# An attention and ternary-FFN block on one core: the hand-written order of every engine's list laid out anew

## The reference

```python
# attention, 16 heads of 16, latent of 64
xn = layernorm(x)
q = xn @ Wq
latent = (xn @ Wk + xn @ Wv) @ W_down_kv
k, v = latent @ W_up_k, latent @ W_up_v
scores = clip(q k^T / 16) * exp(-1e-4 * |i - j|)
y = softmax(clip(scores)) v @ Wo
x1 = x + layernorm(y)
# feed-forward: Hadamard turn, 4-bit activations, ternary weights
xh = layernorm(x1) @ H
s = max(|xh|) / 7 per token
z = clip(round(xh / s), -8, 7) * s @ ternary(weight).T
out = x1 + layernorm(z)
```

## Time and profile before

| | |
|---|---|
| time, median of 3 runs | 1435.21 (1431.94 to 1436.89) |
| profiled execution, time and span | 1435.05, span 1433.2 |
| mean granted TensorE clock | 0.983 |
| busy: PE, DVE, ACT, POOL | 1349.5, 1179.9, 1098.2, 834.7 |
| first score unit of iterations 0, 16, 31 | 33.72, 701.38, 1331.91 |

### The profile page before, as it was taken

How to read it: one execution, slowest core, us unless ns; L and a number is a source line. 1 busy time by engine, 2 the same in 40 slices (tenths; PEclk the granted TensorE clock), 3 DMA queues, 4 the chain that set the end, 5 groups by cost and what they waited for, 6 DMA issues and landing times.

```text
span 1433.2 us, 35971 instructions
## 1 busy us (share of the span) xinstructions
PE 1349.5 (94%) x12330; PEld 600.5 (42%) x12330; DVE 1179.9 (82%) x2739; ACT 1098.2 (77%) x1125; POOL 834.7 (58%) x1238
## 2 busy tenths in 40 slices
PE   5889999999999999999999999999999999999863
PEld 3334444444444444444444444444444444443332
DVE  7567888888888888888888888888888888888655
ACT  1878787888888788878878887887888787787831
POOL 4223655666565666556557655656765655675446
PEclk9999999999999999999999999999999999999986
DMA  6455456556555645656564565655556555555420
GB/s 194 154 167 170 154 172 202 155 164 206 164 182 173 197 156 166 206 157 190 173 190 157 173 201 157 193 175 187 156 177 194 163 185 184 176 156 175 128 77 31
DMA packets 174557, 241.45 MB, mean 168 GB/s; under 512 B 28336, under 2 KB 145200, under 8 KB 174512
## 3 DMA queue, kind: packets, MB, share of 16 engines
q1 hardware_dynamic: 140176, 206.78, 46.5%
q10 hardware_dynamic: 34336, 34.08, 7.7%
HBM read 154.80 MB, written 69.21 MB: 156 GB/s over the span
## 4 chain that ended last, share of the span: by engine, by line
PE 76%; DVE 8%; issue 5%; ACT 4%; DMA 3%; SPq 2%; POOL 2%; DVEq 0%; ACTq 0%; POOLq 0%
PE heads_ps L720 27%; PE scores_ps L707 16%; PE misc_ps L603 8%; PE misc_ps L635 7%; PE misc_ps L660 4%; PE misc_ps L614 3%; PE misc_ps L587 3%; ACT probs L909 2%; DVE x_hl L1204 2%; PE misc_ps L595 2%; PE misc_ps L678 2%; DVE diagonal L1253 2%; DVE weighted L1161 2%; PE misc_ps L625 2%; PE misc_ps L669 1%
## 5 line engine op out<-in xcount | busy, mean ns | idle before, releaser
L909 ACT ACTIVATE probs<-scores_ps 128x1024 f32<-128x1024 f32 x768 | 759.8, 1026 | 248.0 <-PE scores_ps L707 247.9
L720 PE MATMUL heads_ps<-probs,v_sb 128*32 128x512 f32 x4096 | 525.4, 603 | 3.6 <-DVE heads L1150 1.9
L1253 DVE TENSOR_TENSOR diagonal<-scores_ps,comp 128x1024 f32<-128x1024 f32 x256 | 312.2, 1219 | 70.1 <-PE scores_ps L707 70.1
L707 PE MATMUL scores_ps<-q_rep,k_rep 64*128 64x128 f16 (+2 forms) x5120 | 324.6, 251 | 16.0 <-DVE diagonal L1253 9.2
L707 PEld LDWEIGHTS scores_ps<-q_rep,k_rep 64*128 64x128 f16 x5120 | 165.6, 94 | 348.7 <-DVE diagonal L1253 149.5
L916 ACT ACTIVATE probs<-diagonal 128x2048 f32<-128x2048 f32 x128 | 246.0, 1922 | 0.0
L996 POOL TENSOR_TENSOR ln_neg_mean<-zero,ln_moments 128x4 f32<-128x4 f32 (+1 forms) x131 | 34.6, 264 | 356.5 <-DVE ln_moments L1115 356.3
L1161 DVE SCALAR_TENSOR_TENSOR weighted<-misc_ps,edges 128x384 f32<-128x384 f32 x256 | 129.4, 547 | 64.3 <-PE misc_ps L603 33.8
L720 PEld LDWEIGHTS heads_ps<-probs,v_sb 128*32 128x32 f32 x4096 | 91.5, 108 | 171.7 <-issue 169.8
L1038 POOL TENSOR_TENSOR q_hl<-weighted,q_hl 128x768 f16<-128x768 f32 x64 | 105.5, 1648 | 77.5 <-DVE q_hl L1168 77.5
L1043 POOL TENSOR_TENSOR heads_c<-heads_c,den_spread 128x1024 f32<-128x1024 f32 (+1 forms) x33 | 75.7, 2296 | 111.0 <-DMA den_spread<-den_scratch 111.0
(11 more groups left out here) (132 smaller groups left out, 1511.5 us busy)
## 6 DMA issues: line engine op xcount, KB each, us to landing
q_rep<-q_scratch SPq DMA_DIRECT2D x128, 384.0 KB, 4.3
k_rep<-k_scratch SPq DMA_DIRECT2D x256, 192.0 KB, 3.9
q_scratch<-q_hl SPq DMA_DIRECT2D x64, 384.0 KB, 2.6
k_scratch<-k_hl SPq DMA_DIRECT2D x64, 384.0 KB, 3.1
...
heads_c<-heads SPq DMA_DIRECT2D x256, 64.0 KB, 2.5
...
den_spread<-den_scratch SPq DMA_DIRECT2D x256, 64.0 KB, 2.3
```

The source lines that it names most:

```text
L707: ins = mm(scores_ps[:, place + par, at:at + n * P], k_rep[rows, pair, kv_, k_cols], q_rep[rows, pair, qv_, q_cols], start=True, stop=True)
L720: ins = mm(heads_ps[W32 * g:W32 * (g + 1), :], v_sb[:, b.slot, kt, at:at + W32], probs[:, quad % 2, g, kt, :], start=(kt == 0), stop=(kt = ...
L909: nc.scalar.activation(flat[:, :, at:at + S], scores_ps[:, place:place + 2, :], ACT.Exp, scale=EXP_SCALE).then_inc(off_probs, 1)
L1253: v.tensor_tensor(diagonal[:, quad % 2, 2 * two:2 * two + 2, :], scores_ps[:, place:place + 2, :], comp[:].rearrange("p t n -> p (t n)").u ...
```

## The change

No instruction is added or taken away in the iteration; the tables that order them are rewritten, and so are the closing lists.

- PE: the two x1 transposes stand together at step 12. The k parts follow the PV pieces 1 and 2 of quad 0 at steps 14 and 15, the PV piece 3 stands ahead of v at 17. Quad 1's pieces 1 to 3 are one group at step 21. q 1 and y 0 are cut: q piece 0 with y piece 0 at 23, y piece 1 with q piece 1 at 25.
- ACT: the x1T takes are at 12 and 13, the load of x behind the second, all four roundings at 22, the qintT take at 28.
- DVE: xT 0 between the two z takes; lat ahead of the diagonal of step 8; heads_end behind it; z_moments behind x1_low; the quantization ahead of q_split 1, both behind the diagonal of step 24; x_stats ahead of act_scales; heads 1 at 22; y_stats at 29.
- POOL's list of the iteration is the same.
- SP: store_q 0, store_out, store_k 1 and store_q 1 have other places; compaction of half 1 follows the packing of the denominators as before, with no store between.
- The banks come out the same for every piece.
- Closing: on POOL, add_out of batch 29 stands between the two halves of heads_normalize; on SP, the compaction stands ahead of the return; on ACT, the residual load stands behind the first rounding; PE puts qintT between the two halves of y, and some DVE steps change places (that list is left out below).

```diff
 TENSOR_STEPS = {
     1: [("z", 0, 0), ("z", 1, 0), ("pv_end", 3, 0)], 3: [("xT", 0, 0), ("pv_end", 3, 1)], 5: [("xT", 1, 0), ("pv_end", 3, 2)],
-    7: [("pv_end", 3, 3), ("lat", 0, 0)], 9: [("q", 0, 0), ("q", 0, 1)], 11: [("pv", 0, 0), ("x1T", 0, 0)],
-    13: [("x1T", 1, 0), ("pv", 0, 1)], 15: [("k", 0, 0), ("pv", 0, 2), ("k", 1, 0), ("pv", 0, 3)], 17: [("v", 0, 0), ("xh", 0, 0)],
-    19: [("xh", 1, 0), ("pv", 1, 0)], 21: [("pv", 1, 1), ("pv", 1, 2)], 23: [("q", 1, 0), ("q", 1, 1), ("pv", 1, 3)],
-    25: [("y", 0, 0), ("y", 0, 1)], 27: [("pv", 2, 0), ("qintT", 0, 0)], 29: [("y", 1, 0), ("y", 1, 1)],
+    7: [("pv_end", 3, 3), ("lat", 0, 0)], 9: [("q", 0, 0), ("q", 0, 1)], 11: [("pv", 0, 0)], 12: [("x1T", 0, 0), ("x1T", 1, 0)],
+    14: [("pv", 0, 1), ("k", 0, 0)], 15: [("pv", 0, 2), ("k", 1, 0)], 17: [("pv", 0, 3), ("v", 0, 0), ("xh", 0, 0)],
+    19: [("xh", 1, 0), ("pv", 1, 0)], 21: [("pv", 1, 1), ("pv", 1, 2), ("pv", 1, 3)], 23: [("q", 1, 0), ("y", 0, 0)],
+    25: [("y", 0, 1), ("q", 1, 1)], 27: [("pv", 2, 0), ("qintT", 0, 0)], 29: [("y", 1, 0), ("y", 1, 1)],
     31: [("pv", 2, 1), ("pv", 2, 2), ("pv", 2, 3)],
 }
 SCALAR_STEPS = {
-    4: [("load_res", 0)], 12: [("x1T", 0)], 14: [("x1T", 1)], 15: [("load_x", 0)], 21: [("round_x", 0)],
-    22: [("round_x", 1), ("round_x", 2), ("round_x", 3)], 30: [("qintT", 0)],
+    4: [("load_res", 0)], 12: [("x1T", 0)], 13: [("x1T", 1), ("load_x", 0)],
+    22: [("round_x", 0), ("round_x", 1), ("round_x", 2), ("round_x", 3)], 28: [("qintT", 0)],
 }
 VECTOR_STEPS = {
-    1: [("z", 0), ("z", 1), ("x1_make",)], 2: [("xT", 0)], 5: [("x1_stats",), ("xT", 1), ("x1_moments",), ("z_stats",)],
-    8: [("heads_end", 3)], 10: [("lat", 0), ("q_split", 0), ("z_moments",)],
-    15: [("x1_low", 0), ("x1_low", 1), ("k_split", 0), ("den_invert",), ("k_split", 1)], 17: [("v", 0)],
-    18: [("heads", 0), ("act_scales",)], 20: [("v", 1), ("x_stats",), ("x_moments",), ("q_split", 1)], 25: [("heads", 1)],
-    26: [("quantize",)], 27: [("y", 0)], 28: [("y", 1), ("y_stats",), ("y_moments",), ("heads", 2)],
+    1: [("z", 0), ("x1_make",), ("xT", 0), ("z", 1)], 5: [("x1_stats",), ("xT", 1), ("x1_moments",), ("z_stats",), ("lat", 0)],
+    11: [("heads_end", 3), ("q_split", 0)], 13: [("x1_low", 0), ("x1_low", 1), ("z_moments",), ("k_split", 0)],
+    15: [("den_invert",), ("k_split", 1)], 19: [("v", 0), ("heads", 0), ("x_stats",), ("act_scales",)], 20: [("v", 1)],
+    22: [("heads", 1), ("x_moments",)], 24: [("quantize",), ("q_split", 1)], 26: [("y", 0)],
+    29: [("y", 1), ("y_stats",), ("y_moments",)], 30: [("heads", 2)],
 }
 POOL_STEPS = ["x1_apply", ("q", 0), "rstd4", "add_out", ("k", 0), "heads_normalize", ("k", 1), "x_apply", ("q", 1), "rstd2"]
-SYNC_STEPS = [("own", "spread", 1), ("a", "gather_den"), ("a", "pack_den"), ("pre", "store_q", 0), ("a", "compact", 1),
-              ("a", "return_den"), ("a", "spread_den"), ("pre", "store_k", 0), ("pre", "spread", 0), ("own", "compact", 0),
-              ("pre", "store_q", 1), ("pre", "store_k", 1), ("c", "store_out")]
+SYNC_STEPS = [("own", "spread", 1), ("a", "gather_den"), ("a", "pack_den"), ("a", "compact", 1), ("a", "return_den"),
+              ("a", "spread_den"), ("pre", "store_q", 0), ("c", "store_out"), ("pre", "store_k", 0), ("pre", "spread", 0),
+              ("pre", "store_k", 1), ("own", "compact", 0), ("pre", "store_q", 1)]
 
 TENSOR_CLOSING = [
     ("z", 3, None, 0, 0), ("pv_end", 1, None, 3, 0), ("pv_end", 1, None, 3, 1), ("pv_end", 1, None, 3, 2), ("pv_end", 1, None, 3, 3),
-    ("z", 3, None, 1, 0), ("x1T", 2, None, 0, 0), ("x1T", 2, None, 1, 0), ("xh", 2, None, 0, 0), ("xh", 2, None, 1, 0),
-    ("y", 1, 0, 0, 0), ("y", 1, 0, 0, 1), ("y", 1, 1, 1, 0), ("y", 1, 1, 1, 1), ("qintT", 2, None, 0, 0), ("z", 2, None, 0, 0),
+    ("x1T", 2, None, 0, 0), ("x1T", 2, None, 1, 0), ("z", 3, None, 1, 0), ("xh", 2, None, 0, 0), ("xh", 2, None, 1, 0),
+    ("y", 1, 0, 0, 0), ("y", 1, 0, 0, 1), ("qintT", 2, None, 0, 0), ("y", 1, 1, 1, 0), ("z", 2, None, 0, 0), ("y", 1, 1, 1, 1),
     ("z", 2, None, 1, 0), ("x1T", 1, 0, 0, 0), ("x1T", 1, 1, 1, 0), ("xh", 1, 0, 0, 0), ("xh", 1, 1, 1, 0), ("qintT", 1, 0, 0, 0),
     ("z", 1, 0, 0, 0), ("qintT", 1, 1, 0, 0), ("z", 1, 1, 1, 0),
 ]
 SCALAR_CLOSING = [
-    ("x1T", 2, None, 0), ("load_res", 1, None, 0), ("x1T", 2, None, 1), ("round_x", 2, None, 0), ("round_x", 2, None, 1),
+    ("x1T", 2, None, 0), ("x1T", 2, None, 1), ("round_x", 2, None, 0), ("load_res", 1, None, 0), ("round_x", 2, None, 1),
     ("round_x", 2, None, 2), ("round_x", 2, None, 3), ("qintT", 2, None, 0), ("x1T", 1, 0, 0), ("x1T", 1, 1, 1), ("round_x", 1, 0, 0),
-    ("round_x", 1, 0, 1), ("round_x", 1, 1, 2), ("round_x", 1, 1, 3), ("qintT", 1, 0, 0), ("qintT", 1, 1, 0),
+    ("round_x", 1, 0, 1), ("round_x", 1, 1, 2), ("qintT", 1, 0, 0), ("round_x", 1, 1, 3), ("qintT", 1, 1, 0),
 ]
...
 POOL_CLOSING = [
-    ("x1_apply", 2, None), ("rstd4", 3, None), ("add_out", 3, None), ("heads_normalize", 1, 0), ("heads_normalize", 1, 1),
+    ("x1_apply", 2, None), ("rstd4", 3, None), ("heads_normalize", 1, 0), ("add_out", 3, None), ("heads_normalize", 1, 1),
     ("rstd2", 1, 0), ("rstd2", 1, 1), ("x1_apply", 1, 0), ("x1_apply", 1, 1), ("rstd4", 2, None), ("add_out", 2, None), ("rstd4", 1, 0),
-    ("rstd4", 1, 1), ("add_out", 1, 0), ("add_out", 1, 1),
+    ("add_out", 1, 0), ("rstd4", 1, 1), ("add_out", 1, 1),
 ]
 SYNC_CLOSING = [
-    ("gather_den", 1, None), ("pack_den", 1, None), ("return_den", 1, None), ("compact", 1, None, 1), ("spread_den", 1, None),
+    ("gather_den", 1, None), ("pack_den", 1, None), ("compact", 1, None, 1), ("return_den", 1, None), ("spread_den", 1, None),
     ("store_out", 3, None), ("store_out", 2, None), ("store_out", 1, 0), ("store_out", 1, 1),
 ]
```

More of the change, by code:

```diff
@@ L107 @@
 SCALAR_CLOSING = [
[L108 removed]
+    ("x1T", 2, None, 0), ("x1T", 2, None, 1), ("round_x", 2, None, 0), ("load_res", 1, None, 0), ("round_x", 2, None, 1),
     ("round_x", 2, None, 2), ("round_x", 2, None, 3), ("qintT", 2, None, 0), ("x1T", 1, 0, 0), ("x1T", 1, 1, 1), ("round_x", 1, 0, 0),
[L110 removed]
+    ("round_x", 1, 0, 1), ("round_x", 1, 1, 2), ("qintT", 1, 0, 0), ("round_x", 1, 1, 3), ("qintT", 1, 1, 0),
 ]
 VECTOR_CLOSING = [
[L113 to L117 removed]
+    ("x1_make", 2, None), ("x1_stats", 2, None), ("z", 3, None, 0), ("heads_end", 1, None, 3), ("x1_moments", 2, None),
+    ("den_invert", 1, None), ("z", 3, None, 1), ("x1_low", 2, None, 0), ("z_stats", 3, None), ("x1_low", 2, None, 1),
+    ("z_moments", 3, None), ("act_scales", 2, None), ("quantize", 2, None), ("y", 1, None, 0), ("y_stats", 1, 0), ("y_moments", 1, 0),
+    ("y", 1, None, 1), ("x1_make", 1, 0), ("y_stats", 1, 1), ("y_moments", 1, 1), ("z", 2, None, 0), ("x1_stats", 1, 0),
+    ("x1_moments", 1, 0), ("x1_make", 1, 1), ("z", 2, None, 1), ("x1_stats", 1, 1), ("x1_moments", 1, 1), ("z_stats", 2, None),
     ("z_moments", 2, None), ("x1_low", 1, 0, 0), ("x1_low", 1, 1, 1), ("act_scales", 1, 0), ("act_scales", 1, 1), ("quantize", 1, 0),
[L119 removed]
+    ("z", 1, None, 0), ("z_stats", 1, 0), ("z_moments", 1, 0), ("quantize", 1, 1), ("z", 1, None, 1), ("z_stats", 1, 1),
     ("z_moments", 1, 1),
```

6 lines of the change are left out of this document (removed).

## The result

**1479.31** (median of 4 runs, 1469.62 to 1487.16) against 1435.13 for the kernel before in the same comparison (1431.94 to 1436.89): ratio 1.031 [1.024, 1.037]. Slower by 3%, where 1425 was forecast, and outside the range. The runs of the new kernel lie 1.2% apart, those of the old one 0.3%. The profiled execution took 1469.62, its span 1467.8, at a mean granted clock of 0.974. It is the fastest of the four; the slowest, 1487.16, has the lowest mean clock, 0.967.

The account below looks back on a forecast made before the run. PE, busy 94%, was taken as the bound, an iteration being its pieces, switches and a few waits. 30 iterations x (41.94 - 41.5) = 13.2 less, closing 3.5 more: 9.7 less, forecast 1425; own range 1417 to 1433, overall 1412 to 1442.

Parts of the forecast that it names:

- PE's layout: PE's new list laid out with measured start-to-start distances: 16.5 to first k, 13.6 to first y, 11.4 to the end, 41.5.
- PE's own work from k to y, 13.2, and the wait of 0.4: First k part to first y piece: PE's pieces sum to 13.2, the denominator chain to 13.6, so y waits 0.4.
- the rival without the wait at y: The spread lands 0.4 earlier, so y does not wait: iteration 41.1, 25 less and 3.5 more, 1413; chance 0.13.
- group of 24 at 2.71: Expected sign in the profile: three PV pieces in one group of 24 at 2.71, in the middle of an iteration too.
- The casts of q that lasted 1.06: DVE casts of q slowed by a running Pool subtraction; moved behind the diagonal, so this jitter, 41.94 against 41.8, goes.
- 0.7 late for the rounding: Pool's subtraction of k ends 1.2 later, at t 26.4, with DVE's xscale wanted at 25.8, so xscale is 0.7 late.
- The three PV pieces at step 21 hide it: PE's three PV pieces cover the 0.7 by which xscale is late: iteration stays 41.5; uncovered it would be 42.2.
- The chain to y: Denominators from first k through den_inv, return DMA, spread DMAs 2.87 later and Pool product to y: 13.59, taken as 13.6 after.
- I take 0: SP's reordered list costs nothing: last spread issue near t 32, landing by 37.5, PE wants it at 41.5.
- The rival on the slow side: Chain to y gets longer, Pool's product late: 1.0 more an iteration gives 1455, 0.5 more 1440; chance 0.18.
- The closing: After the loop, add_out between the heads_normalize halves and the earlier compaction make it 3.5 later; bounds 0 to 6.
- or 1433 if only one does: Rival of waits coming back ahead of first k: two of 0.2 an iteration give about 1437, one 1433; chance 0.19.

Follow-up runs that it names:

- experiment 9: Changed kernel with the squaring moved behind the quantization, SP's old loop list and the old closing lists: 1417.95, ratio 0.987 to the kernel before.
- experiment 7: Experiment 1 with the third PV piece of quad 1 moved back from step 21 to the end of step 23: 1447.28, ratio 1.007 to the kernel before.
- experiment 1: Changed kernel with DVE's squaring of the four scales moved behind the quantization, step 24: 1425.03, ratio 0.991 to the kernel before.
- experiment 2: Changed kernel with SP's old loop list, all else new: 1423.09, ratio 0.990 to the kernel before.
- experiment 8: Experiment 1 with all five closing lists of the kernel before: 1418.96, ratio 0.988 to the kernel before.

## Why the prediction was wrong

Point by point, by its own steps.

- *PE's layout* was right to 0.1. In iteration 15 of the changed kernel the first k part starts at t 16.48 (said: 16.5), the first y piece at 30.16 (30.1), and the iteration ends at 41.52 (41.5). Here is PE at its k parts in iteration 16; the waits of the earlier trace rows at L614 are gone and from k part to k part it takes 1.87, one score unit and one PV piece between them:

```profile
728.96 0.70 PE L614 MATMUL misc_ps<-latT,w_up_k 64*128 64x256 f32 x4
...
730.83 0.70 PE L614 MATMUL misc_ps<-latT,w_up_k 64*128 64x256 f32 x4
```

- *PE's own work from k to y, 13.2, and the wait of 0.4.* In iteration 15, 13.68, with no wait at y, but 0.30 in front of v for `weighted`, a wait that my layout had put at 0 to 0.2 of room. In iteration 16 of experiment 9 it is 13.34, with neither wait, and the shortest iterations there are 41.11, the 41.1 of the rival without the wait at y. My 41.5 was right in sum partly by luck: the 0.4 came from another wait than the one I had named.
- *The "group of 24 at 2.71"*: right (699.60 - 696.88 = 2.72), and experiment 7 shows that it pays.
- *The casts of q that lasted 1.06*: right. After, 62 of the 64 take 0.56; before, 27 of them took 0.6 or more.
- *The later subtraction of k, xscale "0.7 late for the rounding"*: the meeting came, somewhat smaller. xscale takes 0.67 in place of 0.17, 0.5 more, and by itself it is hidden behind the three PV pieces (experiments 1 and 2).
- **The step that failed is what follows from it in the paragraph on the long iterations: "The three PV pieces at step 21 hide it", and the sum "stays 41.5 as long as the three PV pieces cover it".** I priced the meeting of POOL and DVE for one pair, the subtraction of k with xscale, and put every other meeting at nothing without looking. Behind xscale stand the reciprocal, the squaring and the diagonal, and on POOL the product of 2.35, which I had at t 27.7 with the subtraction ending at 26.4. With 1.3 between the two I did not ask what would happen if the product came sooner. In iteration 16 the product starts at t 26.59 and the squaring at 26.79. The missing term is 2.05 on DVE (2.18 - 0.13) in 20 iterations of 26; on PE it is 1.7, and 3.3 where the clock falls.
- *The chain to y, with 2.87 from return to spread kept as it was*: this is how that step came to fail. The 2.87 became 1.48, so the spread starts at t 21.0 and not at 22.2 as in my sum, and the product at 26.6 and not at 27.7. For SP's list I had written "I take 0", and I looked at it only for what it makes late; it made the spread 0.7 earlier (experiment 2). I had this as the rival without a wait at y, worth 12 us to the good. Its premise came true and its sign was wrong: the earlier spread gains nothing, for with the later one of experiment 2 y hardly waits either (three times in iterations 4 to 29, 1.4 in all), and it brings the product onto the squaring.
- *The rival on the slow side*, a longer chain to y, didn't occur: PE waited at y for the heads 5 times, 4.7 us in all, and only once in iterations 4 to 29 (0.27). So the 0.4 of wait at y in my sum was not there either. I had the right family (POOL pushed later by rstd4 and add_out) with the wrong victim, and 0.18 for it.
- *The closing*: forecast 3.5 longer. Against its like (experiments 1 and 8) it is 3.6; in the changed kernel itself the last stretch is only 2.0 longer than before, and why it is shorter there than in experiment 1 (103.38 for 106.28) is open. add_out (from 1424.77 to 1429.38) stands between the products, as said; POOL's timeline of the closing, answers to the earlier trace rows:

```profile
1423.37 1.26 POOL L1043 TENSOR_TENSOR heads_c<-heads_c,den_spread 128x512 f32<-128x512 f32 x1 [0.92 <-DMA den_spread<-den_scratch]
...
1429.33 1.72 POOL L1043 TENSOR_TENSOR heads_c<-heads_c,den_spread 128x512 f32<-128x512 f32 x1
```

- *The rivals' sums*: "or 1433 if only one does" is a slip; one wait of 0.2 gives 41.7 an iteration, 30 x 0.24 = 7.2 less and 3.5 more, 1431.
- *The sum*, with the one term taken out: experiment 1 has 1425.03, the forecast was 1425. That it fits so well is partly luck, by the 0.4 above. The one instruction that no step named turned -10 into +44.
